# A chain of cross-attention layers: key tiles 4 and 5 in three fp16 products, a Newton step for the reciprocals of the sums

## What is computed

```
q, k, v = x @ Wq, ctx @ Wk, ctx @ Wv          # 16 heads of 64
logits  = q k^T / 8 + col_bias                # -20*(1-mask) on four token columns
out     = softmax(logits) @ v
x       = out @ Wo + bo + x
```

## Time and profile before

| | |
|---|---|
| median of 3 runs | 3433.31 us (3433.30 to 3434.82) |
| profiled execution | 3431.57 us, span 3429.4 us |
| granted TensorE clock, mean | 0.996 |
| busy: PE, DVE, ACT, POOL | 3297.0 (96%), 2537.5 (74%), 2194.5 (64%), 2497.7 (73%) us |
| transfers | 12 GB/s on average |

### The profile page before, as it was taken

How to read it: one execution, slowest core, us unless ns; L and a number is a source line. 1 busy time by engine, 2 the same in 40 slices (tenths; PEclk the granted TensorE clock), 3 DMA queues, 4 the chain that set the end, 5 groups by cost and what they waited for, 6 DMA issues and landing times.

```text
span 3429.4 us, 72971 instructions
## 1 busy us (share of the span) xinstructions
PE 3297.0 (96%) x28066; PEld 1558.9 (45%) x28066; DVE 2537.5 (74%) x4678; ACT 2194.5 (64%) x2698; POOL 2497.7 (73%) x1206
## 2 busy tenths in 40 slices
PE   6999999999987888889999999999999999999998
PEld 3444545445432322234454544445444544445553
DVE  6677877777766788856787777777667777777776
ACT  5466666666545677764666666666546666666665
POOL 6888888888741000028888888888888888888887
PEclk9999999999998999999999999999999999999999
DMA  4000000000000000000000000000000000000000
GB/s 157 1 11 11 1 11 11 11 2 9 6 10 12 8 13 17 17 1 11 11 1 11 11 11 2 11 11 11 1 11 11 1 11 11 11 2 11 3 2 26
DMA packets 50195, 42.29 MB, mean 12 GB/s; under 512 B 4928, under 2 KB 42176, under 8 KB 49856
## 3 DMA queue, kind: packets, MB, share of 16 engines
q1 hardware_dynamic: 49136, 37.08, 3.6%
q10 hardware_dynamic: 720, 0.53, 0.1%
HBM read 32.36 MB, written 2.10 MB: 10 GB/s over the span
## 4 chain that ended last, share of the span: by engine, by line
PE 90%; ACT 3%; DVE 3%; issue 2%; POOL 2%; DMA 0%; SPq 0%; ACTq 0%; DVEq 0%; POOLq 0%
PE ps_j L903 39%; PE ps_st L1054 13%; PE ps_j L1094 11%; PE ps_j L1107 6%; PE ps_sm L986 6%; PE ps_st L1039 3%; PE ps_j L1081 3%; ACT pt L1582 2%; PE ps_sm L1068 2%; PE ps_j L1140 1%; PE ps_st L986 1%; POOL acc L742 1%; PE ps_j L995 1%; PE ps_j L1156 1%; PE ps_j L1131 0%
## 5 line engine op out<-in xcount | busy, mean ns | idle before, releaser
L742 POOL TENSOR_TENSOR acc<-acc,pt 128x1024 f32<-128x1024 f32 x570 | 1365.0, 2395 | 261.9 <-ACT pt L1582 207.2
L1582 ACT ACTIVATE pt<-ps_st 128x1024 f32<-128x1024 f32 x768 | 742.9, 1019 | 300.8 <-PE ps_st L1054 288.9
L2045 DVE CUSTOM_DVE_ANT_0 ps_sm<-ps_sm,bias_m,nmx 128x512 f32<-128x512 f32 x666 | 479.9, 756 | 185.3 <-PE ps_j L986 149.3
L903 PE MATMUL ps_j<-w_h,ctx_h 128*128 128x128 f16 x3072 | 530.5, 219 | 2.3 <-ACT rinv L1598 1.1
L903 PE MATMUL ps_j<-w_l,ctx_h 128*128 128x128 f16 x3072 | 529.4, 219 | 0.0
L903 PE MATMUL ps_j<-w_h,ctx_l 128*128 128x128 f16 x3072 | 529.4, 219 | 0.0
L2045 DVE CUSTOM_DVE_ANT_0 ps_sm<-ps_sm,bias_m 128x512 f32<-128x512 f32 x486 | 334.7, 707 | 158.6 <-PE ps_j L986 147.3
L1094 PE MATMUL ps_j<-pt,v 128*64 128x512 f32 x1792 | 409.2, 598 | 1.3 <-DVE q_l L1933 1.3
L771 POOL TENSOR_TENSOR o_un<-o_un,rinv 128x512 f32<-128x512 f32 x111 | 142.0, 1280 | 336.9 <-ACT rinv L1594 291.1
L2082 DVE RECIPROCAL rinv<-rinv 128x256 f32<-128x256 f32 x190 | 331.3, 1746 | 14.1 <-ACT rinv L1598 4.4
L2035 DVE TENSOR_REDUCE nmg<-ps_st 128x2 f32<-128x1024 f32 x248 | 296.0, 1218 | 45.2 <-PE ps_st L986 43.8
(11 more groups left out here) (201 smaller groups left out, 6603.0 us busy)
## 6 DMA issues: line engine op xcount, KB each, us to landing
w_raw<-wk SPq DMA_DIRECT2D x25, 256.0 KB, 2.9
pt<-ctx_t SPq DMA_DIRECT2D x6, 1024.0 KB, 7.2
w_raw<-wv SPq DMA_DIRECT2D x24, 256.0 KB, 3.6
wo_raw<-wo SPq DMA_DIRECT2D x28, 128.0 KB, 2.0
w_raw<-wq SPq DMA_DIRECT2D x24, 128.0 KB, 3.0
k_h<-k_l SPq DMA_DIRECT2D x72, 32.0 KB, 2.0
x<-x_t SPq DMA_DIRECT2D x4, 512.0 KB, 8.3
acc<-ctx_t SPq DMA_DIRECT2D x2, 1024.0 KB, 9.1
```

The source lines that it names most:

```text
L742: G.tensor_tensor(total, first, pt[:, n % RING, :], ALU.add).then_inc(s_acc, 1)
L903: done = MM(dst, l, r, start=first and i == 0, stop=last and i == n - 1)
L1582: A(pt[:, n % RING, :], src.rearrange("p h q -> p (h q)"), ACT.Exp).then_inc(s_exp, 1)
L2045: last = V.tensor_tensor_reduce(out=src, in0=src, in1=bias_m[:, t, half * HALF:(half + 1) * HALF], scale=-1.0, scalar=nmx[:, 0, t, h:h + 1 ...
```

## The change

In the slots of `thirds`, tiles 4 and 5 are attended in three fp16 products too (`attend_later`), and tiles 6 and 7 stay in fp32 and go first. ScalarE makes the leading halves of the two tiles (`later_lead`), of which tile 4's goes where the fp32 values of tiles 0 to 3 would be and tile 5's into the `p_h` of tile 1; GpSimd makes their rests (`later_rest`). The values of tiles 4 and 5 are split as well: ScalarE copies them apart from those of 6 and 7, and VectorE makes the rest (`later_values_lo`); TensorE waits for it (`s_v_l1`) before it reuses the bank of `v1`.

The third addition moves from GpSimd to VectorE (`add_from_psum`), which reads the tile from PSUM between its two rests. The rest of the sums moves from GpSimd to VectorE in the slots of `early_sums`; GpSimd waits for it where it made it.

The reciprocals of `refined` pairs (90) go: ScalarE takes `Ln` of the sums into `ps_sm` and then `Exp` of its negative there (`guess`), and VectorE makes one Newton step in two instructions (`refine`), which gives the negative of the reciprocal; `add_out` turns the sign. TensorE waits for `s_rinv` before block 2 writes `ps_sm`. One activation table that is to serve both functions is loaded at the start.

The diff, without the declarations of semaphores:

```diff
@@ -208,6 +208,21 @@
     return sum(thirds(q) for q in range(p))
+def early_sums(p):
+    return not grouped(p) and turned(p + 1) and not splits_x(p + 1)
+def refined(p):
+    return not grouped(p) and turned(p + 1)
+def refined_before(p):
+    return sum(refined(q) for q in range(p))
@@ -567,10 +587,21 @@
-            if kt == 0:
+            if kt in (0, 4):
                 return p_l[:]
-            home = kt - 1 if kt == 1 else kt
+            home = kt - 1 if kt in (1, 5) else kt
             return pt[:, (units(p) + home) % RING, 0:TQ].bitcast(F16)
+        def lead_of(p, kt):
+            if kt == 4:
+                return v32[:, p % 2, 0:4, :].rearrange("p k d -> p (k d)").bitcast(F16)
+            return p_h[:, kt % 4, :]
+        def halves_of_values(p):
+            both = v32[:, p % 2, 4:6, :].rearrange("p k d -> p (k d)").bitcast(F16)
+            return [both[:, i * 2 * P:(i + 1) * 2 * P].rearrange("p (k d) -> p k d", d=P) for i in range(2)]
@@ -749,6 +780,16 @@
+            def later_rest(p, kt):
+                pool.wait_ge(s_p_h1, 2 * thirds_before(p) + kt - 3)
+                if kt == 5:
+                    pool.wait_ge(s_acc, ADDS * wides(p) + 4)
+                    pool.wait_ge(s_p_l1, 2 * thirds_before(p) + 1)
+                else:
+                    pool.wait_ge(s_pva, wides(p) + 1)
+                G.tensor_tensor(rest_of(p, kt), pt[:, (units(p) + kt) % RING, :], lead_of(p, kt), ALU.subtract
+                                ).then_inc(s_p_l1, 1)
             def sums_lo(p):
@@ -811,14 +852,16 @@
                     split_x_hi(layer_of(s + 2), batch_of(s + 2))
-                if past and split_sums(s - 1):
+                if past and early_sums(s - 1):
+                    pool.wait_ge(s_acc_l, splits(s - 1) + 1)
+                elif past and split_sums(s - 1):
                     sums_lo(s - 1)
...
                     add(s, 2)
-                if turned(s):
+                if turned(s) and not thirds(s):
                     add(s, 3)
@@ -840,8 +883,12 @@
                         add_bo(layer_of(s), batch_of(s))
+                    if thirds(s):
+                        later_rest(s, 4)
                     add(s, 6)
                     add(s, 7)
+                    if thirds(s):
+                        later_rest(s, 5)
                 if grouped(s + 1) and has_values(s + 1):
@@ -876,6 +923,8 @@
                             pe.wait_ge(s_v_l, thirds_before(m) + 1)
+                        elif thirds(m):
+                            pe.wait_ge(s_v_l1, thirds_before(m) + 1)
                     elif before in ("k0", "k1"):
@@ -1083,8 +1132,39 @@
+            def attend_later(p):
+                done = thirds_before(p)
+                pe.wait_ge(s_exp, units(p) + 8)
+                pe.wait_ge(s_v_sb, values_before(p) + 2)
+                dst = take("pvb", p)
+                for kt in (6, 7):
+                    for h in range(2):
+                        MM(dst[h * HD:(h + 1) * HD, :], values_of(p)[:, kt, h * HD:(h + 1) * HD],
+                           pt[:, (units(p) + kt) % RING, h * TQ:(h + 1) * TQ], start=kt == 6, stop=False)
+                lead, rest = halves_of_values(p)
+                def product(v, weights, kt, stop=False):
+                    for h in range(2):
+                        last = MM(dst[h * HD:(h + 1) * HD, :], v[:, kt - 4, h * HD:(h + 1) * HD],
+                                  weights[:, h * TQ:(h + 1) * TQ], start=False, stop=stop)
+                    return last
+                pe.wait_ge(s_p_h1, 2 * done + 2)
+                pe.wait_ge(s_v_l1, done + 1)
+                for kt in (4, 5):
+                    product(lead, lead_of(p, kt), kt)
+                    product(rest, lead_of(p, kt), kt)
+                for kt in (4, 5):
+                    pe.wait_ge(s_p_l1, 2 * done + kt - 3)
+                    last = product(lead, rest_of(p, kt), kt, stop=kt == 5)
+                last.then_inc(s_pvb, 1)
             def attend(p, part):
+                if part and thirds(p):
+                    attend_later(p)
+                    return
                 pe.wait_ge(s_exp, units(p) + 4 * part + 4)
@@ -1275,6 +1355,8 @@
                     extra_scores(s, i)
+                    if i == 2 and past and refined(s - 1):
+                        pe.wait_ge(s_rinv, 2 * wides(s - 1) + 2)
                     opening, n = next(places), block_bias(s, i)
@@ -1550,12 +1632,27 @@
                 to = v_h[:, p % 2] if thirds(p) and not half else values_of(p)[:, half * 4:half * 4 + 4, :]
-                A(to, bank(f"v{half}", p).rearrange("p (k d) -> p k d", k=4), ACT.Copy, scale=VS / WS).then_inc(s_v_sb, 1)
+                src = bank(f"v{half}", p).rearrange("p (k d) -> p k d", k=4)
+                if thirds(p) and half:
+                    A(halves_of_values(p)[0], src[:, 0:2, :], ACT.Copy, scale=VS / WS)
+                    to, src = to[:, 2:4, :], src[:, 2:4, :]
+                A(to, src, ACT.Copy, scale=VS / WS).then_inc(s_v_sb, 1)
+            def later_lead(p, kt):
+                n = units(p) + kt
+                act.wait_ge(s_exp, n + 1)
+                if kt == 5:
+                    act.wait_ge(s_pva, wides(p) + 1)
+                else:
+                    reaches(act, s_pvb, wides(p))
+                A(lead_of(p, kt), pt[:, n % RING, :], ACT.Copy).then_inc(s_p_h1, 1)
...
                 reaches(act, s_pva, wides(p))
+                if kt == 1:
+                    reaches(act, s_pvb, wides(p))
                 A(p_h[:, kt, :], pt[:, n % RING, :], ACT.Copy).then_inc(s_p_h, 1)
@@ -1597,6 +1694,14 @@
+            def guess(p):
+                p_max, u = passes(p + 1)[3][-1]
+                act.wait_ge(s_sum_sb, p + 1)
+                act.wait_ge(s_max, units(p_max) + u + 1)
+                A(ps_sm[:, 0], rinv[:], ACT.Ln).then_inc(s_log, 1)
+                act.wait_ge(s_log, refined_before(p) + 1)
+                A(ps_sm[:, 0], ps_sm[:, 0], ACT.Exp, scale=-1.0).then_inc(s_guess, 1)
             def reciprocals_out(p):
@@ -1661,6 +1766,7 @@
+            nc.scalar.preload_act_table_set("natural_log_exp_and_others")
             for dst, name in ((tok_i, "tokens"), (mask_t, "masks"), (flags[:], "flags"), (iota[:], "iota"),
@@ -1790,6 +1896,8 @@
                     queries_hi(s + 2)
+                if past and refined(s - 1):
+                    guess(s - 1)
                 if thirds(s):
@@ -1807,7 +1915,11 @@
                     weights_hi(set_of(s) + 1)
+                if thirds(s):
+                    later_lead(s, 4)
                 first_half_out(s)
+                if thirds(s):
+                    later_lead(s, 5)
                 block_bias_out(3)
@@ -2018,6 +2130,17 @@
+            def later_values_lo(p):
+                dve.wait_ge(s_v_sb, values_before(p) + 2)
+                lead, rest = halves_of_values(p)
+                split_lo(rest, bank("v1", p).rearrange("p (k d) -> p k d", k=4)[:, 0:2, :], VS / WS, lead).then_inc(s_v_l1, 1)
+            def add_from_psum(p, kt):
+                total = acc[:, p % 2, :]
+                dve.wait_ge(s_p_e, 2 * thirds_before(p) + kt - 1)
+                dve.wait_ge(s_acc, ADDS * wides(p) + kt - 1)
+                V.tensor_tensor(total, ps_st[:, kt % 2].rearrange("p h q -> p (h q)"), total, ALU.add).then_inc(s_acc, 1)
             def weights_lo_of(p, kt):
@@ -2066,6 +2189,10 @@
+            def sums_lo(p):
+                dve.wait_ge(s_acc_h, splits(p) + 1)
+                V.tensor_tensor(acc_l, acc[:, p % 2, :], acc_h, ALU.subtract).then_inc(s_acc_l, 1)
             def second_half(p):
@@ -2080,6 +2207,12 @@
                 V.reciprocal(r, r).then_inc(s_rinv, 1)
+            def refine(p):
+                dve.wait_ge(s_guess, refined_before(p) + 1)
+                V.tensor_tensor(rinv[:], ps_sm[:, 0], rinv[:], ALU.mult).then_inc(s_rinv, 1)
+                dve.wait_ge(s_rinv, 2 * wides(p) + 1)
+                V.scalar_tensor_tensor(rinv[:], rinv[:], -2.0, ps_sm[:, 0], ALU.add, ALU.mult).then_inc(s_rinv, 1)
@@ -2087,7 +2220,8 @@
                 xs = x32[:, c, batch_of(p) * TQ:(batch_of(p) + 1) * TQ]
-                V.scalar_tensor_tensor(xs, bank(f"out{c}", p), 1 / (WS * VS), xs, ALU.mult, ALU.add).then_inc(s_x, 1)
+                scale = (-1 if refined(p) else 1) / (WS * VS)
+                V.scalar_tensor_tensor(xs, bank(f"out{c}", p), scale, xs, ALU.mult, ALU.add).then_inc(s_x, 1)
@@ -2209,25 +2343,24 @@
                     keys_lo(s + 2, 0)
+                if past and early_sums(s - 1):
+                    sums_lo(s - 1)
                 if past and not grouped(s - 1):
...
                 peak()
-                if past and not grouped(s - 1):
-                    reciprocal(s - 1, 0)
                 if far:
                     queries_lo(s + 2)
-                if thirds(s):
-                    reciprocal(s - 1, 1)
+                if past and refined(s - 1):
+                    refine(s - 1)
                 if far and not splits_x(s):
...
```

(5 more changed lines are left out.)

5 lines of the change are left out of this document (added).

## The result

The changed kernel takes 3557.27 us (median of 4 runs, 3556.37 to 3557.89), the kernel before 3433.31 (median of 4, one more than above, 3432.93 to 3434.82): a ratio of 1.036 (95% interval 1.034 to 1.038), 124 us slower. I had forecast 3522 and slower, within 3455 to 3585. The span of its profiled execution is 3555.4 us, 126.0 more than before.

A forecast was written before the change was run, and what follows sets the result against it. TensorE, busy 96%, was taken as the bound: 78 x (0.4 + 1.1 - 0.435) = 83, plus 6, is 89 us on 3431.6, so 3521, median 3522. Own range 3490 to 3560 (0.68); with (c) and (d), 3455 to 3585 (0.83).

The forecast's parts named there:

- TensorE's own work: TensorE, key tiles 4 and 5: fp32 products (1.79 us) replaced by twelve fp16 (1.355), saving 0.435 us a slot.
- The wait before block 2: TensorE's peak product waits for VectorE's second key rest, behind ScalarE's late exponential and the addition: 1.1 us a slot.
- rival (c): VectorE's addition from PSUM costs as two SBUF inputs do, 2.00 us: 61 us more, 3583; chance 0.08.
- The wait at the start of the slot: TensorE waits for VectorE's values' rest before reusing the bank of `v1`: 0.4 us a slot.
- The fourth slots: 20 slots where VectorE splits weights: GpSimd addition up to 3.42 instead of 2.35 us, 0.3 us waiting, 6 in all.
- The other slots: 12 slots with the new reciprocal but no thirds, layer starts, grouped layer: zero, between -5 and +10 us.
- (a): TensorE's cover holds, VectorE ends key rest and values' rest in time: 34 us less, 3398, faster; chance 0.06.
- (b): Only the end-of-slot wait for the values' rest appears: -3 us, 3429 to 3435; chance 0.07.
- (e): ScalarE's `Ln` and `Exp` each load their own table: 201 us more, 3722; chance 0.04.
- (d): GpSimd's rest of tile 5 ends last in every slot, by up to 0.4 us: 23 more, 3545; chance 0.07.

The follow-up runs named there:

- the two combinations: Changed kernel, third addition back on GpSimd, output weights' rest moved, logarithm before query copy, block 0 peak products after four score products: 3481.1 us; with VectorE adding tile 2: 3478.4.
- The parts alone: Kernel before with one part each: refinement alone 3430.1 us, third addition on VectorE alone 3464.2 us, tiles 4 and 5 in three fp16 products alone 3501.2 us.

## Why the prediction was right, and what was off

**TensorE's own work** was right: eight fp32 instructions in 1.87 us and twelve fp16 in 1.29 by the chain after, together 3.16 where 3.58 stood; the saving of 0.435 is 0.42, and the changed kernel with its addition back on GpSimd (saving and slot-start wait, -0.01 us a slot) fits it together with the slot-start wait.

**The wait before block 2** was the step that decided, and it held with its reason: ScalarE late by guess, VectorE's addition behind the last exponential, the key rest behind that. I had 1.1 us and it was 1.23. The terms: the logarithm took 0.60 (I had 0.63), and the next copy started 0.49 after the start of the exponential (I had 0.5); the second exponential in PSUM ended at 15.9 us of the slot, as I had it; the addition took 1.22, as taken from the rows with a PSUM input (the far end of 2.00, and so rival (c), is out); and the rest behind it started 0.12 us after its end where I had 0.03. Refinement and addition without the tiles, 1.22 us in 75 of 78 slots, show this term by itself.

**The wait at the start of the slot** was forecast at 0.4 and measured at 0.39. But I counted it as a price of its own, and without it the slot gets only 0.06 shorter: GpSimd's rest of tile 5 stands right behind. I had seen that with 0.5 us to spare; the trace of the changed kernel has the rest end at 5.09 us (forecast 4.95) and TensorE asking at 5.40 (5.5), 0.3 us.

**The fourth slots** are the term that was mis-sized: 6 us in my sum, 24 measured (20 x (2.34 - 1.13)), and 7 more in the six token-row slots, which the sum did not have. A fourth slot is 1.06 us longer than an ordinary one. The long addition was there as forecast, but I had 0.3 us for it and it alone is 0.71: TensorE gets to the product with the rest of tile 5 0.5 us late (of which 0.36 show in the list of waits, 7.2 us in 20 times), and the late rest then holds up VectorE's sums' rest and what stands behind it. I had taken that meeting as covered, and in the ordinary slots it is: the sums' rest takes 1.46 us in place of 1.21 there and nobody waits. What I missed altogether is that the rest of the output weights after the second peak now stands beside GpSimd's rest of tile 5, which is the remaining 0.35. I had the rule in hand and applied it to `sums_lo` alone. The Trainium skill, SBUF — State Buffer, section Who interferes with whom, has it: a VectorE instruction with two SBUF inputs contends with a GpSimd instruction that reads SBUF. This trace agrees, with 2.13 us in place of 0.42 for the rest of the output weights and 2.17 in place of 1.28 for the token rows, and 0.42 again once GpSimd's rest was away. I should have asked it of every VectorE instruction with two SBUF inputs in the stretch that GpSimd's new rest moved into, not of those the change touches.

**The other slots**, which I took at zero between -5 and +10, gave 4.2 and 2.0 us.

**Rivals.** (a) and (b) needed the wait before block 2 to stay away, and it did not. (e) did not happen: the logarithm and the exponential follow each other within 0.63 us, 90 times, with no load between, and the loads around the grouped layer are gone. (d), GpSimd's rest last in every slot, is wrong for the changed kernel (20 waits, not 78). It came true in experiments: 76 such waits without the values' rest and in each of the two combinations, 75 with the tiles alone.

**The sum.** 78 x 1.13 = 88 (forecast 83), 31 for fourth and token slots (6), 6 elsewhere (0): 125 against 89. The result lies inside the forecast's own range (3490 to 3560), but by 3 us, and the width that let it in was set for the two waits; that the miss in the fourth slots fell within it is luck. The parts alone (-3, +31 and +68) make 96 and the change 124: refinement and addition cost 94 together, where they cost 28 apart, and the rest of the change adds 30 to that instead of the tiles' 68, since, by the counts above, the helpers have made room on GpSimd by then. How much of that room is owed to which helper was not run.

## What to carry to other kernels

Spare time in front of the bound engine is a budget that several edits share: work out what each leaves of it, because the first looks free and the last pays for all. An operation handed to a helper engine is worth its length only where the helper's inputs are early; behind the last input of a stretch it goes on the path in full (1.2 us here), and with another tile of the same sum it may not (0.23 us). When GpSimd gets new work, look at every VectorE instruction with two inputs from SBUF that runs beside it, moved or not: here one of 0.42 us became 2.13.

## What the runs showed of the hardware that I had not expected

A VectorE instruction of 0.42 us with two inputs from SBUF that starts 0.28 us after a GpSimd instruction of 2.15 us ends 0.28 us after it, and is recorded as 2.15 us long (rows above): by these times its record holds the waiting, and the next VectorE instruction starts only at its end (583.65). Between two VectorE instructions of which the second waits for the first, the gap was 0.12 us with the addition in PSUM ahead (564.23 to 564.35), not the 0.03 to 0.04 of the two in the Newton step (559.44 to 559.48) or of the chain in the root mean squares. ScalarE's exponential of 128x512 from PSUM to PSUM took 0.582 us, and its logarithm from SBUF to PSUM 0.597, where the exponential from SBUF to SBUF takes 0.63.
